# Adding the causal mask on VectorE while it takes the row maxima, for chunks of two key blocks

## The reference

```python
x = layernorm(x + attn_A(x))          # 16 query heads of size 8, ONE key/value head, rotary, causal
x = layernorm(x + ffn(x))
# ffn(x): h = x + attn_B(rmsnorm(x, g1))   16 query heads of size 64, 4 key/value heads, rotary, causal
#         h + moe(rmsnorm(h, g2))          8 experts, top 2, capacity n/8, hidden 256
# both attentions:
scores = where(key <= query, q @ k.T, -inf) / sqrt(d)
p = softmax(scores)                    # subtracts the maximum of each row
```

## Time and profile before

| | |
|---|---|
| median of 3 runs | 534.98 us (533.77 to 535.16) |
| the profiled execution | 533.74 us |
| its span, first to last instruction | 531.9 us |
| TensorE matmuls, busy | 462.6 us (87%), 2980 |
| VectorE | 368.0 us (69%), 1023 |
| ScalarE | 229.1 us (43%), 418 |
| GpSimd | 161.7 us (30%), 200 |
| mask products L715, 256 columns / 512 columns | 128, 281 ns recorded / 64, 387 ns recorded |
| maxima L1371, two-block / one-block | 128 / 64, all 0.68 to 0.69 us recorded |
| mean granted TensorE clock | 0.968 |

### The profile page before, as it was taken

The page is one execution under the profiler, slowest core; times in us unless marked ns, Lnnn a source line. Parts: engine busy times, 40 slices in busy tenths (PEclk is TensorE's granted clock), DMA queues, the critical chain, the costliest instruction groups (busy, mean ns, idle before and its releaser), DMA issues.

```text
span 531.9 us, 8374 instructions
## 1 busy us (share of the span) xinstructions
PE 462.6 (87%) x2980; PEld 259.6 (49%) x2980; DVE 368.0 (69%) x1023; ACT 229.1 (43%) x418; POOL 161.7 (30%) x200
## 2 busy tenths in 40 slices
PE   3877976899999999999999999999988969888930
PEld 2544533455365555735563655445344427565620
DVE  3634789947777786788579777847984536655785
ACT  1262531754474175337443742654243330545531
POOL 4311130510423132225303331403403646061542
PEclk9987899999999999999999999999999999899985
DMA  7600000000021003000300120030080162023224
GB/s 207 201 2 2 1 3 0 3 1 1 4 49 33 2 4 81 1 2 3 81 1 4 32 50 2 5 81 0 7 234 2 44 155 97 1 76 100 62 68 99
DMA packets 19095, 23.95 MB, mean 45 GB/s; under 512 B 2630, under 2 KB 15374, under 8 KB 18158
## 3 DMA queue, kind: packets, MB, share of 16 engines
q1 hardware_dynamic: 15308, 18.29, 12.8%
q0 software_dynamic: 1648, 4.07, 2.8%
q10 hardware_dynamic: 2098, 1.05, 0.7%
HBM read 16.81 MB, written 6.28 MB: 43 GB/s over the span
## 4 chain that ended last, share of the span: by engine, by line
PE 65%; DVE 17%; issue 5%; DMA 5%; ACT 5%; POOL 2%; ACTq 1%; POOLq 0%; DVEq 0%
PE ps_r L1003 7%; PE ps_r L1027 7%; PE ps_st L968 5%; PE ps_r L715 5%; PE ps_st L1273 4%; PE ps_r L773 4%; PE ps_r L873 4%; DMA xs_dram<-x_all,sidx 3%; PE ps_st L957 3%; PE ps_r L1016 3%; PE ps_r L850 3%; DVE rmax_a L1371 2%; PE ps_r L823 2%; PE ps_r L982 2%; PE ps_r L832 2%
## 5 line engine op out<-in xcount | busy, mean ns | idle before, releaser
L606 POOL TENSOR_TENSOR qkr<-qkr,prod 128x512 f32<-128x512 f32 (+1 forms) x48 | 52.3, 1095 | 182.9 <-DVE prod L1497 182.7
L1371 DVE TENSOR_REDUCE rmax_a<-ps_r 128x2 f32<-128x512 f32 (+1 forms) x96 | 62.2, 686 | 46.1 <-PE ps_r L850 45.9
L1371 DVE TENSOR_REDUCE rmax<-ps_r 128x2 f32<-128x512 f32 (+1 forms) x96 | 62.4, 685 | 16.7 <-PE ps_r L982 12.4
L715 PE MATMUL ps_r<-cbt 128*128 128x256 bf16 (+1 forms) x192 | 60.7, 316 | 3.6 <-ACT xT_b L1969 1.1
L1954 ACT ACTIVATE pt<-ps_st 128x1024 f32<-128x1024 f32 x48 | 46.9, 1018 | 35.9 <-PE ps_st L968 35.9
L643 POOL TENSOR_TENSOR oT<-pvb,oT 128x1024 f32<-128x1024 f32 x14 | 32.8, 2369 | 67.9 <-DMA oT<-inv_dram 67.9
L1945 ACT ACTIVATE pt<-ps_st 128x1024 f32<-128x1024 f32 x48 | 46.5, 1024 | 12.7 <-PE ps_st L757 12.5
L2015 ACT ACTIVATE pvb<-ps_r 128x512 f32<-128x512 f32 x32 | 19.0, 596 | 72.8 <-PE ps_r L1003 72.6
L1003 PE MATMUL ps_r<-pt,vb 128*64 128x512 f32 x192 | 48.2, 608 | 2.3 <-ACT pt L1954 2.0
L1027 PE MATMUL ps_r<-wqkv,xT_b 128*128 128x512 f32 x96 | 48.1, 605 | 1.0 <-DVE prod L1497 0.5
L715 PEld LDWEIGHTS ps_r<-cbt 128*128 128x128 bf16 x192 | 18.4, 96 | 48.9 <-issue 32.8
(11 more groups left out here) (238 smaller groups left out, 869.3 us busy)
## 6 DMA issues: line engine op xcount, KB each, us to landing
oT<-inv_dram SPq DMA_DIRECT2D x14, 512.0 KB, 5.7
xs_dram<-pvb SPq DMA_DIRECT2D x1, 2048.0 KB
pt<-in_L_ffn_w SPq DMA_DIRECT2D x2, 1024.0 KB, 7.4
ys_dram<-qkr SPq DMA_DIRECT2D x14, 128.0 KB, 1.9
qkr<-xs_dram POOLq DMA_DIRECT2D x4, 256.0 KB, 3.8
x_all<-in_L_attn_x ACTq DMA_DIRECT2D x1, 896.0 KB, 8.9
pvb<-xs_dram POOLq DMA_DIRECT2D x3, 256.0 KB, 4.9
out<-x_all SPq DMA_DIRECT2D x1, 640.0 KB, 3.8
```

The lines of the kernel that those rows point to most:

```text
L606: nc.gpsimd.tensor_tensor(part, part, prod[:, (3 * t + i) % 2, 0:w], ALU.add).then_inc(add_in, 1)
L715: nc.tensor.matmul(o[:, :, P * (i >= 4):], ident_b, qmask.unsqueeze(1).broadcast_to([P, heads, P]), start=True, stop=False, skip_group_che ...
L1371: nc.vector.tensor_reduce(heads_of(i), ps_r[:, b, :].rearrange("p (h k) -> p h k", h=4 if i < 4 else 2), AX.X, ALU.max).then_inc(free[b], 1)
```

## The change

Two-block chunks no longer get a mask product; their score product starts the bank. VectorE takes each of the two heads by a tensor_tensor_reduce over 256 columns: it adds `both_masks` (a new bf16 table: 128 columns of zeros, then `qmask`), writes the sum back into the same PSUM columns, and takes the maximum into rmax. One-block chunks keep the mask product and the reduce. The tile `tmap` (30 numbers) moves into free columns of another tile, and the bf16 table grows by 128 columns.

```diff
-    b = np.concatenate([np.eye(P), add_row, by_query, by_key, np.ones((P, P)), tri, top_row, by_strip], 1)
+    b = np.concatenate([np.eye(P), add_row, np.zeros((P, P)), by_query, by_key, np.ones((P, P)), tri, top_row, by_strip], 1)
...
+        both_masks = cbt[:, CB_BOTH:CB_BOTH + T]
...
-        tmap = sb("tmap", [P, sum(COUNT)], mybir.dt.int32)
+        tmap = late[:, 800:800 + sum(COUNT)].bitcast(mybir.dt.int32)
...
                 o = fill(s, name)
-                heads = 4 if i < 4 else 2
-                o = o.rearrange("p (h k) -> p h k", h=heads)
-                nc.tensor.matmul(o[:, :, P * (i >= 4):], ident_b, qmask.unsqueeze(1).broadcast_to([P, heads, P]),
-                                 start=True, stop=False, skip_group_check=True)
+                o = o.rearrange("p (h k) -> p h k", h=4 if i < 4 else 2)
+                if i < 4:
+                    nc.tensor.matmul(o, ident_b, qmask.unsqueeze(1).broadcast_to([P, 4, P]), start=True, stop=False,
+                                     skip_group_check=True)
                 return o
...
-                    nc.tensor.matmul(o, q, k, start=False, stop=True, skip_group_check=True).then_inc(full, 1)
+                    nc.tensor.matmul(o, q, k, start=i >= 4, stop=True, skip_group_check=True).then_inc(full, 1)
...
                         mm = nc.tensor.matmul(o, qhi[1 - u][:, i - 4, P:], kdiag[1 - u][:, i % 2, :, :],
-                                              start=False, stop=True, skip_group_check=True)
+                                              start=True, stop=True, skip_group_check=True)
...
                     b = filled(dve, s, f"{name}{i}")
-                    nc.vector.tensor_reduce(heads_of(i), ps_r[:, b, :].rearrange("p (h k) -> p h k", h=4 if i < 4 else 2),
-                                            AX.X, ALU.max).then_inc(free[b], 1)
+                    to, o = heads_of(i), ps_r[:, b, :].rearrange("p (h k) -> p h k", h=4 if i < 4 else 2)
+                    if i < 4:
+                        ins = nc.vector.tensor_reduce(to, o, AX.X, ALU.max)
+                    else:
+                        for h in range(2):
+                            ins = nc.vector.tensor_tensor_reduce(o[:, h, :], o[:, h, :], both_masks, 1.0, 3 * NEG, ALU.add,
+                                                                 ALU.max, to[:, h:h + 1])
+                    ins.then_inc(free[b], 1)
```

More of the change, by code:

```diff
@@ L187 @@
 CF = CF_PLACES + sum(COUNT)
-CB_ID, CB_ADD, CB_QMASK, CB_KMASK, CB_ONES, CB_TRI, CB_TOP = (P * i for i in range(7))
-CB_STRIPS = 7 * P
+CB_ID, CB_ADD, CB_BOTH, CB_QMASK, CB_KMASK, CB_ONES, CB_TRI, CB_TOP = (P * i for i in range(8))
+CB_STRIPS = 8 * P
 CB = CB_STRIPS + 4 * P
```

## The result

The changed kernel takes 543.23 us (median of 4 runs, 542.74 to 544.68) against 534.38 of the kernel before in the same session (533.25 to 535.16): **ratio 1.0172, 95% interval [1.0143, 1.0201]**, that is 1.4 to 2.0% slower. The profiled execution took 543.14 us, its span is 541.2 us against 531.9.

What follows compares the result with a forecast made beforehand. TensorE and VectorE were taken to bound steady steps in turn, VectorE the opening. Steps 0 to 4 -2.3, opening +1.5, step -1 +0.4, step 5 0, step 6 +0.4: 0.0 us, so 535.0 us, range 530.5 to 544.

Steps and rivals of the forecast that it cites:

- the case it stood on: Whole kernel: a chunk price on VectorE of 0.66 to 0.72 us gives 531.5 to 537.5 us; chance 0.75.
- a start-to-start time above 0.37: New sums on VectorE: they should start 0.34 to 0.35 us apart; above 0.37 would show the forecast wrong.
- I take 0.345 for one, 0.69 for the chunk: 0.09 more than the reduce: VectorE, each two-block chunk: two sums with accumulator reads cost 0.69 us, against 0.60 for the reduce.
- the third rival: VectorE's sums: reading and writing the same PSUM bank halves the rate, 1.20 us a chunk, 580 us in all; chance 0.04.
- Sum: 0.35 + 0.11 = 0.46 a step: Steps 0 to 4: 0.35 us gained by am8 and 0.11 at p12, 2.3 us over five steps.
- VectorE starts bm4 at 220.01 whatever TensorE does: Ahead of bo0: VectorE's start after the layer norm is fixed, so bo0 gains 0.15 us, not 0.48.
- The mechanism of a step: Steady step: VectorE gapless from am8 to p02's rotation, TensorE waiting on it ahead of bo0, p01 and bv3.
- Opening, +1.5: Opening, where VectorE is the chain: two-block chunks at the higher price, less one mask, lose 1.5 us.
- step -1, +0.4: Step -1: bm4 and bm5 delay p00, later chunks delay p10; 0.4 us lost.
- Step 6, +0.4: Routing step: six reduces in a row at 0.09 us more each, less one mask, lose 0.4 us.
- The sums hold back their successors: am8 to bm9 and opening: each instruction starts only at its predecessor's recorded end; 541 to 547 us; chance 0.13.
- TensorE keeps the gain: Steady steps: VectorE's idle time takes the additions, five steps gain 1.9 us each, 527.5 us; chance 0.08.

Runs made afterwards that it cites:

- e1: The changed kernel, with the opening's sums written to an SBUF tile instead of back into PSUM; 549.10 us in one run.
- e6: The changed kernel, with two plain maxima over 256 columns in place of the two sums, causal mask left out; 543.96 us in one run.
- e5: The changed kernel, with one plain 512-column maximum per two-block chunk and no causal mask there; 541.39 us, ratio 0.9965.
- e7: The kernel before, with VectorE masking only chunks am0 to am3 from step 0 on; 533.57 us, ratio 0.9983.
- e8: The changed kernel, with two-block mask products issued again before step 0 and overwritten by the score product; 544.11 us, ratio 1.0019.

## Why the prediction was wrong in its sum

The range (530.5 to 544) held the result, 543.2, with 0.8 us to spare; that is luck as much as foresight, for the forecast of 535.0 and the case it stood on (531.5 to 537.5, chance 0.75) both missed. The price came out 0.074 higher in series. By the 0.9 us for each 0.01 that makes 6.7 us, and 9.3 were measured between the spans. A sign of being wrong that the prediction had named, a start-to-start time above 0.37, was met. Point by point:

- **The price, "I take 0.345 for one, 0.69 for the chunk: 0.09 more than the reduce".** This step failed. The row behind it, the mean square, writes SBUF. e1 gives exactly 0.345 for that, and the changed kernel 0.382 once sums in a series go to PSUM. I had named the PSUM write as unseen, but priced it only as the catastrophe of the third rival (580 us), with nothing between. The release, "0.69 + 0.08", is about 0.76 + 0.14 = 0.90.
- **"Sum: 0.35 + 0.11 = 0.46 a step".** Mis-sized beyond the price. At 0.66 a chunk I gave 0.8 a step; e6 measures 0.47 (2.37 over five). At 0.60, e5 measures 0.72. Between e6 (0.66) and the changed kernel (0.76, 0.47 lost) a straight line has 0.2 a step won at 0.69 (an estimate from these two), where I said 0.46. The masks were taken as 0.12 us of TensorE's time each, but those of bm8 and bm9 lay in a wait for ScalarE. Another thing the walk left out is the lock: I took "VectorE starts bm4 at 220.01 whatever TensorE does" as fixed, while that start is set by GpSimd's end, by a DMA's landing, and moved by up to 0.7 us between steps of the changed kernel.
- **The mechanism of a step** held: VectorE gapless from am8 to p02's rotation and beyond, TensorE waiting for it ahead of bo0 (0.24 us) and bv3 (0.16), though not ahead of p01, and ahead of nm1 (0.24), which I had not named.
- **Opening, +1.5, and step -1, +0.4.** The same chunks at 0.16 instead of 0.09 make 18 x 0.16 - 0.12 = 2.8 and 0.7, together 3.5. Measured within a session: 3.7, 6.3 and 7.3. The price accounts for the first; what adds to it in the other two stays open. The fall of TensorE's clock was not foreseen; e5 had it in part, and its opening was no longer.
- **Step 6, +0.4.** Here the price scales cleanly: six chunks at 0.16 are 1.0, and nmT of step 6 is 1.0 later against step 6's start (it starts 10.13 us later than before, the step 9.14). *Step 5*, put at 0, is 0.48 longer (37.59 against 37.11). The work behind takes part of both back, for all behind step 4 is only 0.6 longer.
- **The rivals.** "The sums hold back their successors" has the right side and time (541 to 547) and its point of decision, 0.72, was passed, but not by its mechanism: no instruction waits for its predecessor's recorded end (0.47 recorded, 0.38 to the next). So the rule of the Trainium skill (VectorE: DVE Perf Modes, "The DRAIN you can't avoid") that the next op waits for the pipe to empty, taken as I took it, is not borne out either; the same section adds that a next op which is not held starts earlier, and that is what the rows show. "TensorE keeps the gain" is out: even e5, with no price at all, keeps 3.6 of 9.6 us. The halved rate is out.

## What to carry to other kernels

When the nearest row for a new operation differs from it in one operand's memory, keep a middle value in the sum for that difference, not only a far end: here it was 0.04 us on 256 instructions, many of them on a chain. Work that one engine gives up has to go where the other idles, chunk by chunk: the same instruction that loses 1.7% when it takes every two-block chunk made steps 0 to 4 shorter by 3.4 and 4.9 us of 240 when it was put only where VectorE had gaps, with the lock eased. And before a fixed start is used as an anchor, ask what sets it: a two-column instruction that lasts over a microsecond is waiting for something.

## What the runs showed of the hardware that was not expected

- VectorE tensor_tensor_reduce, 128x256, PSUM source and bf16 mask: 0.345 us from start to start with the sum in SBUF (e1), 0.382 with the sum in PSUM behind another such one (changed kernel); accumulator read 0.08 against 0.14. At 128 columns into PSUM 0.25 in a series (e7).
- A 128x512 maximum costs 0.60 us from start to start, two of 256 columns 0.66 (e6).
- VectorE instructions of 2 to 4 columns lasted 0.5 to 2.4 us and ended within 0.03 us of a GpSimd 128x1024 product; with that product moved, 0.17.
- With the mask products gone, TensorE was granted 0.59 from 22 to 26 us, mostly 1.2 GHz, where it had 2.4 before, with VectorE's sums (changed kernel) and without them (e5); with the products put back as filler (e8) it had 1.00.
